# GpSimd waits for its landed gathers ahead of every eighth one, in a two-layer graph kernel

## The reference

```
h = relu(layernorm(x))
# layer 0: GraphSAGE with a maximum, S = 25
idx  = the 25 lowest neighbours of each node          # top_k over -arange, where adj != 0
agg  = max over the neighbours of h[idx]               # rows beyond the degree count as 0
x    = x + relu(concat(h, agg) @ W + b)
h = relu(layernorm(x))
# layer 1: graph attention with one head
hid  = h @ W1.T ;  s = leaky_relu(a1.hid_n + a2.hid_m, 0.2)
x    = x + softmax(s where adj > 0) @ hid + bias
```

## Time and profile before

| | us |
|---|---|
| median of 3 runs without a profile | 4273.25 (4268.43 to 4274.99) |
| span of the profiled execution | 5229.9 |
| GpSimd busy / its idle time ahead of gathers | 3055.8 / 1944.2 |
| first and last gather start at | 38.3 and 4999.5 |
| VectorE busy, TensorE busy, ScalarE busy | 2599.4, 2607.8, 1568.6 |

### The profile page before, as it was taken

How to read it: one execution, slowest core, us unless ns; L and a number is a source line. 1 busy time by engine, 2 the same in 40 slices (tenths; PEclk the granted TensorE clock), 3 DMA queues, 4 the chain that set the end, 5 groups by cost and what they waited for, 6 DMA issues and landing times.

```text
span 5229.9 us, 38170 instructions
## 1 busy us (share of the span) xinstructions
PE 2607.8 (50%) x8674; PEld 1604.8 (31%) x8782; DVE 2599.4 (50%) x6725; ACT 1568.6 (30%) x1745; POOL 3056.0 (58%) x3204
## 2 busy tenths in 40 slices
PE   2122235556455455545555545555554555553479
PEld 0011113333233333333333323333332333332256
DVE  5444354454455454555445546545455554544432
ACT  3011123323333323333323333332333333232135
POOL 5565556666666566666656666666666665666510
PEclk6555557777666777667777766777766777776689
DMA  7344446556655555565655655665566565555320
GB/s 253 114 162 141 144 139 188 160 181 181 176 180 177 168 178 170 178 189 170 187 155 178 184 178 168 188 178 172 170 178 188 170 187 157 171 175 154 121 88 29
DMA packets 477228, 866.03 MB, mean 166 GB/s; under 512 B 308298, under 2 KB 309204, under 8 KB 456660
## 3 DMA queue, kind: packets, MB, share of 16 engines
q0 software_dynamic: 153600, 419.64, 28.2%
q1 hardware_dynamic: 305140, 378.64, 22.5%
q10 hardware_dynamic: 18432, 67.12, 3.3%
HBM read 690.98 MB, written 119.54 MB: 155 GB/s over the span
## 4 chain that ended last, share of the span: by engine, by line
PE 26%; issue 23%; another core or an unknown queue 22%; DVE 17%; ACT 8%; SPq 2%; DMA 1%; POOL 1%; ACTq 0%; DVEq 0%; POOLq 0%
PE acc L1333 13%; DVE highest L917 6%; DVE lin L941 3%; PE bank L1266 3%; ACT nm_t L566 2%; ACT wgt L602 2%; PE pen L1326 2%; DVE top L851 2%; PE pen L1325 1%; PE bank L1246 1%; DVE key L857 1%; ACT pen L596 1%; PE bank L1283 1%; SPq L364 1%
## 5 line engine op out<-in xcount | busy, mean ns | idle before, releaser
L521 POOL DMA_INDIRECT near<-table_dram,idx x3200 | 3055.8, 955 | 1944.2 <-issue 1000.3
L1333 PE MATMUL acc<-hid,wgt 128*128 (+1 forms) x4096 | 1187.2, 442 | 458.8 <-ACT wgt L602 380.9
L1333 PEld LDWEIGHTS acc<-hid,wgt 128*128 128x128 f32 x4096 | 889.6, 223 | 643.7 <-issue 435.2
L917 DVE TENSOR_TENSOR highest<-near,highest 128x512 f32<-128x512 f32 x1280 | 889.8, 695 | 167.5 <-DVE highest L917 75.9
L933 DVE SCALAR_TENSOR_TENSOR x_q<-bank,x_q 128x256 f32<-128x256 f32 x128 | 54.2, 423 | 1269.6 <-PE bank L1268 1052.9
L602 ACT ACTIVATE wgt<-pen,a_slope 128x512 f32<-128x512 f32 x448 | 305.5, 682 | 984.6 <-remote 522.7
L1266 PE MATMUL bank<-w_sb,h_t 128*128 128x256 f32 x1024 | 381.0, 536 | 422.8 <-ACT h_t L692 314.1
L566 ACT ACTIVATE nm_t<-adj_i,big_c 128x2048 bf16<-128x2048 int32 x128 | 501.1, 3942 | 7.3 <-DMA adj_i<-in_adj_dram 4.8
L941 DVE CUSTOM_DVE_ANT_0 lin<-acc,nm_q 128x2048 bf16<-128x2048 f32 x108 | 247.5, 2291 | 385.6 <-ACT acc L713 382.8
L1275 PE MATMUL acc<-cst,wgt 128*128 128x128 f32 x248 | 61.0, 427 | 750.6 <-ACT wgt L577 680.8
L1266 PEld LDWEIGHTS bank<-w_sb,h_t 128*128 128x128 f32 x1024 | 261.1, 268 | 508.5 <-ACT h_t L692 333.4
(11 more groups left out here) (148 smaller groups left out, 2253.8 us busy)
## 6 DMA issues: line engine op xcount, KB each, us to landing
adj_i<-in_adj_dram SPq DMA_DIRECT2D x128, 1024.0 KB
nmask_dram<-nm_t ACTq DMA_DIRECT2D x128, 512.0 KB
nm_q<-nmask_dram SPq DMA_DIRECT2D x29, 2048.0 KB
near<-table_dram,idx POOLq DMA_INDIRECT x3200
h_q<-table_dram SPq DMA_DIRECT2D x32, 512.0 KB
x_q<-in_x_dram SPq DMA_DIRECT2D x32, 512.0 KB
xmid_dram<-x_q SPq DMA_DIRECT2D x32, 512.0 KB
o_q<-xmid_dram SPq DMA_DIRECT2D x32, 512.0 KB
```

What stands on the lines that cost most here:

```text
L521: pool.indirect_dma_start(out=near[:, t % 2, k, :], out_offset=None, in_=table, in_offset=bass.IndirectOffsetOnAxis(ap=idx[:, t, k:k + 1], ...
L917: nc.vector.tensor_tensor(highest[:, :], pair(k), highest[:, :], ALU.max).then_inc(mx_step, 1)
L1333: mm = nc.tensor.matmul(acc[:, t, 0:C + 1], wgt_part(j)[:, t * P:(t + 1) * P], hid[:, bass.ds(batch * NJ + j, 1), 0:C + 1].rearrange("p a ...
```

## The change

Ahead of each gather (t, k) of a step with k > 0 and 25 t + k a multiple of 8, GpSimd also waits until all gathers of this tile that it has issued so far, 0 to k-1, have landed. That is ahead of (0, 8), (0, 16), (0, 24), (1, 7), (1, 15), (1, 23), (2, 6), (2, 14), (2, 22), (3, 5), (3, 13) and (3, 21). The ties stay. The order of all work stays.

```diff
+PACE = 8
...
+            def landed(s, t, k):
+
+                if k > 0 and (t * S + k) % PACE == 0:
+                    pool.wait_ge(near_in[t % 2], 16 * S * (2 * s + t // 2) + 16 * k)
+                    pool.nop(nofuse=True)
+
             def step(s, lo, stages):
...
                     for k in range(S):
                         attention(s, stages, t, k)
+                        landed(s, t, k)
                         pool.indirect_dma_start(
```

## The result

The changed kernel takes 5534.81 us (median of 4 runs, 5529.69 to 5541.78) beside 4274.12 us of the kernel before (4 runs, 4268.43 to 4275.27): a ratio of 1.2951 [1.2932, 1.2969], 1261 us more. The direction was forecast. The size was not: 4445 us was the forecast, 5050 the top of its range, 5041 to 5279 the span of rival 3.

A forecast was written before the change was run, and what follows sets the result against it. The bound was taken to be the attention and first-layer round on TensorE, ScalarE and VectorE. Waits of 883 + 238 us less 949 us of cover gave +172: 4273 + 172 = 4445 us, range 4215 to 5050.

The forecast's parts named there:

- rival 3: Added waits on GpSimd find no cover and show in full: 5041 to 5279 us; chance 0.21 with what lies towards it.
- reading A: The runs lack the 0.30 us gaps between GpSimd's gathers; 949 us of cover remain, forecast 4445 us at the upper price.
- 906 us of tie waits: GpSimd's profiled waiting for other engines at ties and buffers, 28 us in each of 32 steps.
- the cover: GpSimd's time standing at ties, which added waits would fill unseen: 906 us in the profile, 949 in the runs.
- Reading B: Gathers keep their pace in the runs and other engines are faster; no cover, all of 768 to 1006 us shows.
- sum of 4281 us: 3200 gathers by 0.949 + 0.305 us, 4013 us, with 38 ahead and 230 behind: the whole time.
- in-between case of 1.1 us a gather: Gathers spaced 1.1 us: cover 485 us, a wait 2.15 us, loss +341 to +579 us.
- Quiet drain: Added wait for landing on an uncrowded queue: 2.4 landing + 0.84 waking - 1.25 = 2.0 us, 768 for 384.
- Crowded drains: Added waits ahead of (2, 6) and near (3, 12), amid other transfers: 6.6 and 6.2 us, 238 us more altogether.
- the two places forecast: Waits ahead of (2, 6) and at (3, 12), forecast as the dear ones, 6.6 and 6.2 us.
- Rival 1: All added waits on GpSimd hide in tie waits, which just get shorter: 4273 us; chance 0.13.
- Rival 2: Emptied queues let mask transposes through, halving ScalarE's waits at L596: 4273 - 92 = 4181 us; chance 0.17.

## Why the prediction was wrong

**The step that failed** is "So in the profile GpSimd is not the bound", carried over to the runs by the choice of reading A: "against B, it needs all of 906 us of tie waits to vanish". They do vanish: the 16.5 us left when the kernel before is profiled in an execution as long as its runs are steady gaps, and taking the ties out changes nothing (0.9997). So the cover, 949 us in the forecast's sum, is nothing in the runs. That is 949 of the 1090 us by which 4445 was too low; the rest is the price. Reading B, rival 3, was right about what bounds the kernel, though the 5535 us lie above its range too. Its sum of 4281 us was on the table, 8 from the median, where A had to let the gather's steady gap of 0.30 us disappear for no reason shown; and the earlier trace rows beside the earlier trace rows showed an engine that had stood still. That it came so near is partly luck: the gathers took 4032 us where it has 4013, and the tail 194 where it has 230. Nor are the 1000.3 us of the earlier trace rows all steady gap, as the prediction read them: 2990 x 0.305 is 912 us, and the longest of these gaps is 20.1. (Without weight for the sum: (1, 24) is the third gather behind the one at 2431.20, not the fourth; the time given for it is right.) The in-between case of 1.1 us a gather falls with A: the pace was 1.25 us in both profiles of the kernel before, and between drains in the changed one.

**The price** had the right parts, a quiet drain and the crowd, and was low in the size of both. By B the sum was 768 to 1006 us; 1265 were measured.
- Quiet drain: forecast 2.0 us, measured 2.54 - 0.30 = 2.24, by 384 some 860 us in place of 768. The landing was right, 2438.10 - 2435.69 = 2.41 us. Waking was put too low: from the last packet to the next gather 2439.17 - 2438.10 = 1.07 us pass, not the 0.84 taken from VectorE's semaphore.
- Crowded drains: forecast two a step, in the 27 steps with attention, 4.2 and 4.6 us dearer than quiet ones, 238 us. Three come in nearly every step, 3.7 to 5 us dearer in the stretch shown, and what is left of the 1265 us is 405. They stand at other places, and some in steps without attention (7.30 us in step 0), so "the crowd comes with attention's own progress" does not hold; that the two places forecast land as fast as the rest is the sign that the prediction named for being wrong about the crowd.

Per step the forecast was 24 + 8.8 = 32.8 us; 12 x 3.29 = 39.5 came.

The Trainium skill (DMA: Bandwidth & Descriptors, Anatomy of one DMA) led to an estimate of some 730 us for the 384 waits. The 2.3 us estimated from it for one transfer are near the 2.41 us of the row; the runs show 1265 us in all because waking took longer than the 0.84 us in that estimate, and because the crowd is in no figure for one transfer by itself.

**What would show it.** The list behind the prediction pointed the right way after the event: the runs lost 1261 us where the profiled span lost 5531.5 - 5229.9 = 301.6, which was the sign named for rival 3. GpSimd's waits for near's own DMA came to 1360 us, above the 700 to 1000 named; few tie waits are left, and the wait at the first maximum is far beyond 131 us, as forecast.

**Rival 1** (all hidden) needs cover; with 25 neighbours there is none, with 21 there are 445 us, and 454 us of drains hide in them but for 8 us of time.

**Rival 2** (emptied queues let the mask transposes through): ScalarE's waits for the masks do shrink, in the kernel before (second profile) and the changed one:

```profile
ACT pen L596 <- DMA nm_c<-nm_q: 374.6, 74, 11.6
```

```profile
ACT pen L604 <- DMA nm_c<-nm_q: 301.9, 71, 8.7
```

But the changed kernel is 29% longer, so its transposes have more time anyway. With 96 drains at 21 neighbours the waits go from 363.5 to 347.1 us and the time does not fall. Nothing speaks for the rival.

**What stays open:** why VectorE and the other engines paused in the first profiled execution of the kernel before. It was not seen again, and no run was aimed at it. Nor does a run show what decides which drains meet the crowd.

## What to carry to other kernels

Hold the profiled span against the time of the runs before a wait is counted as cover: where they differ by a fifth, add up each engine's own work at its steady spacing, and if one sum gives the run time, that engine is the first to suspect as the bound, however idle it looks, and a second profile decides. A wait for the transfer just issued costs the landing and the waking less one issue, 2.2 us here on a quiet queue and 3.3 on average, and is paid in full on the longest round; a wait for a group issued eight transfers earlier cost nothing here, since its data had landed each time. What is hidden and what is paid is best told apart by changing the count of the waits, since cover shows as a part that comes free.

## What was not expected of the hardware

The gathers' spacing is very even: 0.95 us busy and 0.30 us to the next, in every profile, with few exceptions (as the 1.97 us ahead of (0, 13) with 768 drains), so 3200 of them take 4032 us though GpSimd counts as busy for only 72% of 4264.7 us. And TensorE's granted clock, as the mean over the span, was lower in the longer executions: 0.745 of full speed without the ties (span 4263.4 us), 0.746 in the second profile of the kernel before, 0.678 in the changed kernel and 0.652 with 768 drains; the same 8674 matmuls are busy for 2616.0 us in the changed kernel and 2431.1 in that second profile. No cost of it shows in the changed kernel's time: TensorE is 4% of its chain, and the 194.0 and 195.5 us behind the last gather are nearly alike.
